# Last layer of a four-layer kernel: search and attention in one fixed alternation, last values of a unit carried into the next

## What is computed

```
q, k, v = x @ Wq.T, x @ Wk.T, x @ Wv.T, split in 16 heads of 16
scores = einsum('bhtc,bhkc->bhtk', q, k) * 16 ** -0.5, causal
attn = softmax(scores, axis=-1)
out = einsum('bhtk,bhkc->bhtc', attn, v)
return out (heads side by side) @ Wo.T
```

## Time and profile before

| | us |
|---|---|
| median of 3 runs | 3845.64 |
| lowest and highest run | 3840.07, 3855.26 |
| span of the profiled execution | 3867.5 |

### The profile page before, as it was taken

How to read it: one execution, slowest core, us unless ns; L and a number is a source line. 1 busy time by engine, 2 the same in 40 slices (tenths; PEclk the granted TensorE clock), 3 DMA queues, 4 the chain that set the end, 5 groups by cost and what they waited for, 6 DMA issues and landing times.

```text
span 3867.5 us, 47778 instructions
## 1 busy us (share of the span) xinstructions
PE 3519.2 (91%) x16468; PEld 2089.1 (54%) x16468; DVE 2473.4 (64%) x6381; ACT 1730.0 (45%) x3237; POOL 1164.8 (30%) x1190
## 2 busy tenths in 40 slices
PE   8899999968898988989878999998899999999998
PEld 7677777734555545545546667676543333433332
DVE  4444443455788988889865443443568788678774
ACT  2234443322234423343344544443346666666667
POOL 0322222151355555555542322223211111011111
PEclk7799999988899999999989999999889899999999
DMA  3244445321466666666750000000101011111100
GB/s 109 73 165 168 177 180 180 128 66 71 136 204 193 216 211 194 197 204 197 212 187 3 0 1 1 1 1 9 38 20 31 20 23 34 31 34 27 32 18 23
DMA packets 107154, 368.87 MB, mean 95 GB/s; under 512 B 27248, under 2 KB 41088, under 8 KB 96928
## 3 DMA queue, kind: packets, MB, share of 16 engines
q0 software_dynamic: 57664, 302.82, 24.3%
q1 hardware_dynamic: 48160, 60.90, 5.6%
q10 hardware_dynamic: 1088, 2.10, 0.2%
HBM read 322.59 MB, written 17.69 MB: 88 GB/s over the span
## 4 chain that ended last, share of the span: by engine, by line
PE 66%; DVE 21%; ACT 6%; issue 4%; another core or an unknown queue 2%; POOL 1%; DMA 0%; POOLq 0%; DVEq 0%; SPq 0%; ACTq 0%
PE ps L184 51%; PE ps L2636 6%; DVE pm L2784 4%; PE ps L1507 2%; DVE mi L1642 2%; DVE gathB L1719 2%; DVE ps L2787 2%; DVE hacc L1682 2%; ACT P L2917 1%; PE ps L2126 1%; DVE mx L1638 1%; PE ps L556 1%; PE ps L581 1%; PE ps L546 1%
## 5 line engine op out<-in xcount | busy, mean ns | idle before, releaser
L2917 ACT ACTIVATE P<-ps 128x512 f32<-128x512 f32 (+3 forms) x1280 | 587.3, 548 | 214.1 <-PE ps L184 212.0
L2784 DVE TENSOR_REDUCE pm<-ps 128x1 f32<-128x512 f32 x768 | 484.6, 684 | 113.3 <-PE ps L184 113.0
L1860 POOL DMA_INDIRECT gathB<-in_tab,idx x256 | 282.9, 1105 | 357.6 <-PE ps L1507 287.4
L184 PE MATMUL ps<-QS,KS 49*128 49x512 f32 (+3 forms) x1280 | 333.8, 422 | 16.2 <-DVE pm L2784 12.6
L1860 POOL DMA_INDIRECT gathA<-in_tab,idx x256 | 268.7, 1049 | 203.2 <-DVE mx L1638 125.5
L184 PE MATMUL ps<-KS,QS 48*128 48x512 f32 (+3 forms) x1280 | 309.8, 430 | 16.0 <-DVE pm L2787 5.9
L2974 POOL TENSOR_SCALAR_AFFINE_SELECT P<-P 128x256 f32<-128x256 f32 x256 | 103.8, 409 | 709.9 <-ACT P L2917 709.0
L2636 PE MATMUL ps<-P,Va 128*32 128x512 f32 (+3 forms) x2560 | 309.7, 557 | 5.8 <-POOL P L2974 2.9
L184 PEld LDWEIGHTS ps<-QS,KS 49*128 49x128 f32 x1280 | 158.2, 190 | 225.0 <-DVE pm L2784 81.8
L184 PEld LDWEIGHTS ps<-KS,QS 48*128 48x128 f32 x1280 | 145.5, 191 | 212.8 <-DVE pm L2784 66.2
L2787 DVE CUSTOM_DVE_ANT_0 ps<-ps,past 128x128 f32<-128x128 f32 (+3 forms) x512 | 240.1, 515 | 26.6 <-PE ps L184 24.6
(11 more groups left out here) (390 smaller groups left out, 7002.8 us busy)
## 6 DMA issues: line engine op xcount, KB each, us to landing
ys_sorted<-moe SPq DMA_DIRECT2D x71, 128.0 KB
KS<-hi SPq DMA_DIRECT2D x256, 32.0 KB, 1.9
QS<-hi SPq DMA_DIRECT2D x256, 32.0 KB, 1.9
gathA<-in_tab,idx POOLq DMA_INDIRECT x256
gathB<-in_tab,idx POOLq DMA_INDIRECT x256
KS<-lo SPq DMA_DIRECT2D x128, 32.0 KB, 1.9
QS<-lo SPq DMA_DIRECT2D x128, 32.0 KB, 2.0
out<-xT SPq DMA_DIRECT2D x8, 512.0 KB, 3.2
```

The costliest lines, as they stand in the source:

```text
L184: m = pe.matmul(out, w, x, start=start and i == 0, stop=stop and i == len(pairs) - 1, skip_group_check=True)
L1860: pool.indirect_dma_start(out=(GA, GB)[half][:, h, :], out_offset=None, in_=d[f"tab{half}"], in_offset=bass.IndirectOffsetOnAxis(ap=idx[t ...
L2784: v = dve.tensor_reduce(m, p, AX.X, ALU.max)
L2917: act.activation(P_[:, hh, off:BW], psx.tile("s2", j, n, kt, pr, hh)[:, off:BW], ACT.Exp).then_inc(*psx.emptied(MN.act, "s2", j, n, kt, pr ...
```

## The change

Search units have 8n + 8 chunks, all 0.125 apart: projection and maxima transpose join the chunk of their step. Attention units have 12n + 12 chunks, three for each key tile, 0.13, 0.04 and 0.08 apart, from 6.02 on. So one order holds throughout while both run: maxima, scores, maxima, scores, values, each group a step. The values of a unit's last key tile are no longer issued at its end but after the scores of the next unit's first tile (`tail.before`). The pieces of `finish` move accordingly: the copy of the output from the unit's end to the second score step of the next unit, the sum matmul from step 1 to 4, the reciprocal from steps 1 and 2 to 5 and 6, the output projections from 6 and 7 to 8 and 9, the additions to x from 6 and 7 to 9 and 10 (what is left after a unit's last step is issued before the first scores of the next). A step of `finish` used to stand ahead of the next chunk's work and now stands behind the scores of its own. GpSimd divides after the diagonal tile 2 instead of 0 where the unit is n = 0. The last piece of the v projection moves to unit (4, 0).

```diff
@@ -2486,7 +2486,8 @@
 
 
 
-            PHASE, PROJECT, SEEK, VALUES, ATTEND = (0.0, 0.055), (0.2, 0.3), 1.0, (4.2, 0.12), 6.0
+            PHASE, PROJECT, SEEK, VALUES, ATTEND = (0.0, 0.055), (0.2, 0.3), 1.0, (4.2, 0.12), 6.02
+            SEARCH, STEP = 0.125, (0.13, 0.04, 0.08)
 
             def at_pace(chunks, step):
                 for _ in chunks:
@@ -2495,12 +2496,13 @@
             def everything(qk, phase, prep, v, main, last):
                 def seek():
                     for u in range(NJ * NQ):
-                        yield from at_pace(prep(*divmod(u, 4)), (u % 4 + 1) / (8 * (u % 4) + 10))
+                        yield from at_pace(prep(*divmod(u, 4)), SEARCH)
                     yield from at_pace(last(), 0.1)
 
                 def attend():
                     for u in range(NJ * NQ):
-                        yield from at_pace(main(*divmod(u, 4)), (u % 4 + 1) / (12 * (u % 4) + 13))
+                        for i, _ in enumerate(main(*divmod(u, 4))):
+                            yield STEP[i % 3]
 
                 def project():
                     for n in range(2):
@@ -2538,7 +2540,7 @@
 
 
                 def __init__(self):
-                    self.gen = iter(())
+                    self.gen, self.before = iter(()), None
 
                 def step(self):
@@ -2607,51 +2609,48 @@
                                 pe.wait_all(psx.freed("s", j, pr, qt, c, hh))
                                 chain(pe, p[hh][:, 0:w], [(Q[rs, pr, qs], K[rs, pr, c * 512:c * 512 + w])]).then_inc(
                                     *PP.pe.tick("s", j, pr, qt, c, hh))
-                            yield
                             step += 1
                             also = beside(n, step)
                             if also == "qk" and ahead(j, n)[0] < NJ:
                                 pe_qk(pe, *ahead(j, n))
                             if also == "max" and preceding(j, n)[0] >= 0:
                                 pe_max(pe, *preceding(j, n))
-                            if also:
-                                yield
+                            yield
 
             def pe_last(pe):
                 pe_max(pe, NJ - 1, NQ - 1)
                 yield
 
+            def pe_values(pe, j, n, kt, off):
+                o_ = po.fill("o", j, n) if kt == 0 else po.tile("o", j, n)
+                if kt == 0:
+                    pe.wait_all(po.freed("o", j, n))
+                pe.wait_ge(*PP.act.has("v", j // 4, 14))
+                pe.wait_ge(*(MN.pool.has("causal", j, n, kt, 1) if kt >= 4 * n else MN.act.has("s2", j, n, kt, 1, 1)))
+                for hd in range(4):
+                    h = 4 * (j % 4) + hd
+                    m = pe.matmul(o_[32 * hd:32 * hd + 32, off:BW], Va[:, kt, h * 17:h * 17 + 32],
+                                  Pb[2 * (kt % 2) + hd // 2][:, hd % 2, off:BW], start=kt == 0, stop=kt == 4 * n + 3,
+                                  skip_group_check=True)
+                m.then_inc(*MN.pe.tick("pv", j, n, kt))
+
             def pe_main(pe, j, n, tail, v):
-                g = j % 4
-                def pv(n, kt, off):
...
-
-                def finish(n):
+                def finish():
+                    yield from nothing(3)
                     p = psx.fill("sum", j, n)
...
-                    yield from nothing(5)
+                    yield from nothing(4)
...
-                before = None
                 for kt in range(4 * n + 4):
                     off = max(0, (kt - 4 * n) * 128)
                     for pr in range(2):
@@ -2664,21 +2663,19 @@
                             chain(pe, s2[hh][:, off:BW], [(K[rs, pr, kt * 128:(kt + 1) * 128],
                                                            Q[rs, pr, n * BW + off:(n + 1) * BW])]).then_inc(
                                 *MN.pe.tick("s2", j, n, kt, pr, hh))
+                        tail.step()
                         yield
-                        tail.step()
-                        if pr == 1 and before is not None:
-                            pv(n, *before)
-                            if kt % 2 and kt > 2:
-                                next(v, None)
-                            yield
-                    before = (kt, off)
-                yield
-                pv(n, *before)
-                for _ in v:
-                    pass
+                    if tail.before is not None:
+                        pe_values(pe, *tail.before)
+                    tail.before = (j, n, kt, off)
+                    if kt % 2 and kt > 2:
+                        next(v, None)
+                    if (n, kt) == (0, 0):
+                        for _ in v:
+                            pass
+                    yield
                 tail.drain()
-                tail.gen = finish(n)
-                yield
+                tail.gen = finish()
@@ -2689,8 +2686,11 @@
                     yield from nothing(TURN)
                     yield from pe_phase(pe)
 
+                second = pe_v(pe, 1)
                 pe_all(pe, everything(lambda j, n: pe_qk(pe, j, n), phase, lambda j, n: pe_prep(pe, j, n), lambda: pe_v(pe, 0),
-                                    lambda j, n: pe_main(pe, j, n, tail, pe_v(pe, 1) if (j, n) == (3, 3) else iter(())), lambda: pe_last(pe)))
+                                    lambda j, n: pe_main(pe, j, n, tail, second if (j, n) in ((3, 3), (4, 0)) else iter(())),
+                                    lambda: pe_last(pe)))
+                pe_values(pe, *tail.before)
                 tail.drain()
@@ -2789,24 +2789,22 @@
                                 v.then_inc(*psx.emptied(PP.dve, "s", j, pr, qt, c, hh))
                             if (qt, c) == (4 * n + 3, n):
                                 dve_maxima(dve, j, n, pr)
-                            yield
                             step += 1
                             also = beside(n, step)
                             if also == "qk" and ahead(j, n)[0] < NJ:
                                 dve_qk(dve, *ahead(j, n))
                             if also == "max" and preceding(j, n)[0] >= 0:
                                 dve_max(dve, *preceding(j, n))
-                            if also:
-                                yield
+                            yield
...
-            def dve_main(dve, j, n, tail, v):
-                def finish(n):
+            def dve_main(dve, j, n, tail):
+                def finish():
                     b = j // 4
-                    yield from nothing(5)
+                    yield from nothing(8)
                     for m in range(2):
                         dve.wait_ge(*MN.pe.has("out", j, n, m))
                         dve.wait_ge(*x_before(4 * b + n))
@@ -2817,18 +2815,11 @@
 
                 for kt in range(4 * n + 4):
                     for pr in range(2):
+                        tail.step()
                         yield
-                        tail.step()
-                        if pr == 1 and kt:
-                            if kt % 2 and kt > 2:
-                                next(v, None)
-                            yield
-                yield
-                for _ in v:
-                    pass
+                    yield
                 tail.drain()
-                tail.gen = finish(n)
-                yield
+                tail.gen = finish()
 
             def dve(dve):
                 dve_start(dve)
@@ -2840,7 +2831,7 @@
                     yield from dve_phase(dve)
 
                 dve_all(dve, everything(lambda j, n: dve_qk(dve, j, n), phase, lambda j, n: dve_prep(dve, j, n), lambda: nothing(8),
-                                    lambda j, n: dve_main(dve, j, n, tail, nothing(8) if (j, n) == (3, 3) else iter(())), lambda: dve_last(dve)))
+                                    lambda j, n: dve_main(dve, j, n, tail), lambda: dve_last(dve)))
                 tail.drain()
 
 
@@ -2886,16 +2877,17 @@
 
             def act_prep(act, j, n):
                 for step in range(1, 8 * n + 9):
-                    yield
-                    also = beside(n, step)
-                    if also == "qk" and ahead(j, n)[0] < NJ:
+                    if beside(n, step) == "qk" and ahead(j, n)[0] < NJ:
                         act_qk(act, *ahead(j, n))
-                    if also:
-                        yield
+                    yield
 
             def act_main(act, j, n, tail, v):
-                def finish(n):
-                    act.wait_ge(*MN.pool.has("on", *((j, n - 1) if n else (j - 1, 3))))
+                def finish():
+                    yield
+                    act.wait_ge(*MN.pool.has("on", *preceding(j, n)))
+                    act.wait_ge(*MN.pe.has("pv", j, n, 4 * n + 3))
+                    act.activation(osb[:, :], po.tile("o", j, n)[:, :], ACT.Copy).then_inc(*po.emptied(MN.act, "o", j, n))
+                    yield from nothing(3)
                     act.wait_ge(*MN.pe.has("sum", j, n))
```

(30 more changed lines are left out.)

13 lines of the change are left out of this document (1 added, 12 removed).

## The result

The changed kernel takes 4013.8 us (median of 4 runs, 4012.2 to 4018.0), the kernel before 3848.3 us beside it. The ratio is 1.042, 95% interval 1.0391 to 1.0448: slower by 166 us, where I had forecast 3858 and a range up to 3893. No other layer moved: what was added lies in the last layer's stage.

A forecast was written before the change was run, and what follows sets the result against it. No engine is full; seven ring banks tie TensorE to VectorE. Terms sum to 122.2 us a turn against 120.6, 1.6 more over 7.8 turns: 3845.6 + 12.5 = 3858 us, range 3793 to 3893 (the forecast's own 3835 to 3881).

The forecast's parts named there:

- terms 1 and 2: Strict rounds: full values 1.00 us, 34.8 a turn; rest of a full round 1.70, 68.0 a turn, less 2.3.
- term 5: Query and key projection after a unit's first maxima: values start 4.1 us after the previous values end; 9.5 a turn.
- Term 3: Sum matmul in key tile 1, in front of the values: nothing to wait for, nothing hiding it; 0.96 each, 3.8 a turn.
- Term 4: Output projection: first half 0.96 us, second 0.69, 6.6 a turn; shorter lead waits 0 to 0.6 a unit, 0.6 a turn.
- The first rival: VectorE becomes the bound of the search and attention stage, full rounds at 2.52 us; 3825, or 3796; chance 0.30.
- my third rival: First output half waits 0.6 us, with VectorE's peaks and the projection's late bank; 3885 likely, 3898 at worst; chance 0.21.
- The clock: Rival over the stage: steadier work returns up to 20 us, chance 0.04, or looser work costs as much, chance 0.03.
- The carried values: At unit ends, save waits for the output's copy (16.3 us) and GpSimd's mask (12.5), 3.7 a turn, already in the sum.
- the sign of that rival: VectorE above 85% busy in a turn, or full rounds of 2.5 us, would prove the first rival.

The follow-up runs named there:

- pace_only: The kernel before with the strict alternation alone, last values still issued at their unit's end and the finish at its old steps; ratio 1.000.
- both_early: The changed kernel with the logarithm at step 4 instead of 5 and the additions at steps 8 and 9 instead of 9 and 10; ratio 1.013.
- filled_wait: The changed kernel with six zero-weight matmuls added in each unit, ahead of the last scores of key tile 2, in the wait for the logarithm; ratio 1.038.
- The single edits: Two runs, each the changed kernel with one edit: logarithm at step 4 instead of 5, ratio 1.024; additions at steps 8 and 9 instead of 9 and 10, ratio 1.031.
- filled_start: both_early with four zero-weight matmuls added ahead of the second score step of each unit; ratio 1.010.
- both_phase: both_early with the alternation turned round to scores, maxima, scores, maxima, values; ratio 0.997.

## Why the prediction was wrong

*The strict rounds* (terms 1 and 2) were right. In the changed kernel full rounds follow each other at 2.70:

```profile
3265.37 1.06 PE L2632 MATMUL ps<-P,Va 128*32 128x512 f32 x8
...
3268.07 1.07 PE L2632 MATMUL ps<-P,Va 128*32 128x512 f32 x8
...
3270.77 1.07 PE L2632 MATMUL ps<-P,Va 128*32 128x512 f32 x8
...
3275.73 0.50 PE L184 MATMUL ps<-QS,KS 49*128 49x512 f32 x1 [0.30 <-DVE lo L2758]
```

and the projection's round that starts at 3270.77 lasted until the next values at 3276.16, 5.39 us where term 5 had 1.00 + 4.1; its last scores waited for the low part, as worked out. Term 5 was 0.3 short, 9 us over the stage. Strictness came out neutral in time (pace_only), where I had a loss of 12.5 us. At the full clock the loss is there: taking 0.4 us off for each us of slow time, an estimate near the slope among repeated runs below, pace_only's span gives 3832 - 160 = 3672 and the kernel before in its runs beside it (3830.4 us at clock 0.945, slow time 421) 3830 - 168 = 3662, 10 us less. The slow time that it saved pays for that (394 us over its runs against 427). I had not foreseen that a denser order is also repaid by the clock.

*Term 3 is the step that failed.* I wrote that the sum matmul comes "in front of the values, where nothing is left to wait but also nothing hides it", and priced 0.96 us. That is only the wait for its fill. I never asked who needs its bank next, though I had named the ring of seven as what ties the engines. The bank comes back with the logarithm, which the diff moves from step 1 to 5 while the sum moves from 1 to 4: held one step longer, and that step holds the values and two exponentials. It cost 3.88 - 2.70 = 1.18 us a unit at the full clock, and 3.17 - 2.47 = 0.70 in the units n = 0, where the scores and values are narrower (after from 3457.95, both_early from 3403.03). That is 23 x 1.18 + 8 x 0.70 = 33 us, taking these rounds for all, without the clock.

*Term 4* made the same error: it priced the second output half as before, at 0.69, and asked only whether its own input would be late. The first rival even counted VectorE's later additions as a lead for VectorE; they hold two ring banks one step longer. The round after the second half takes 3911.58 - 3907.44 = 4.14 us in the changed kernel and 3183.07 - 3179.69 = 3.38 in both_early, so 0.76 a unit or 24 us over 31 units. The wait for GpSimd's product, on which my third rival stood, is small: 16.4 us in 19 waits, and the round with the first half took 3907.44 - 3903.20 = 4.24 against 3.99, and next to nothing more in the units n = 0, so 6 us in all, within the bounds of term 4.

```profile
3903.20 1.07 PE L2632 MATMUL ps<-P,Va 128*32 128x512 f32 x8
...
3907.44 1.06 PE L2632 MATMUL ps<-P,Va 128*32 128x512 f32 x8
...
3911.58 0.64 PE L2632 MATMUL ps<-P,Va 128*32 128x512 f32 x4
```

```profile
3179.69 1.06 PE L2632 MATMUL ps<-P,Va 128*32 128x512 f32 x8
...
3183.07 1.06 PE L2632 MATMUL ps<-P,Va 128*32 128x512 f32 x8
```

*The clock* got a chance of 0.03 to cost something, with no mechanism. It carries a quarter to a half of the loss. The stage's slow time rose by 227 - 79 = 148 us. Among repeated runs of the kernel before, beside pace_only, the fastest (3819.2 us, clock 0.949, slow time 389) and the slowest (3849.6, clock 0.938, 477) differ by 30 us for 88 us of slow time, 0.35 us each; the most that work bound by TensorE can lose at half the clock is 0.5. So 52 to 74 us of the 143 by which the profiled executions differ, an estimate; filled_wait's 0.25 would make it 37. Waits worked out above: 33 + 24 + 6 = 63. That leaves 6 to 28 us, of which the strict order at full clock is some 10; the rest is not attributed. The single edits bear this out: the logarithm's 33 us of waits gave back 70, the additions' 24 gave back 41.

*The carried values* themselves: I let them save the copy's wait, and they did. But with both releases early the carried order is still 1.3% slower. I suspect that it spreads the thin rounds at a unit's start evenly, where the old order issued several maxima in a row; no run tests that alone. filled_start says that a part of this loss is the clock, and both_phase that it can be avoided by the other phase.

*The rivals.* VectorE never became the bound: it was busy 99.4 of 143.4 us, 69% where the sign of that rival was 85%. My third rival had the right sign and kind (a late piece of the finish becomes TensorE's wait), but the wrong piece, and even at its worst (3898) a third of the size.

## What to carry to other kernels

When a piece of work moves in a shared ring of buffers, price two waits: that of its own fill, and that of whoever takes its buffer next. A move of the producer by three steps and of the releasing reader by four isn't neutral. Follow the chain from release back to the fill and see what long instruction lies in it. And a standstill of TensorE that comes back in every unit can cost about twice its own length (33 us of waits, 70 us of time here), if the clock falls with it; read the granted clock of the stage beside every wait, and look also at how evenly an order feeds TensorE, which the third loss suggests and no run here tests alone.

## What the hardware showed that I had not expected

The mean granted clock of one program differs from run to run, and the time goes with it: 13 runs of the kernel before on one chip spread from 3819 to 3850 us as their mean clock went from 0.949 to 0.938. So the profiled execution's slow time is one sample, and a comparison of two kernels by it alone can mislead, as for both_phase. Extra TensorE work that stands in a wait can pay for itself through the clock: 1.5 us of useless matmuls in each of 32 units took away 92 us of slow time and cost nothing net, while without the wait the same matmuls cost 37 us. That they lower the time isn't shown.
